# Reordering the expert-routing work on VectorE inside an attention loop

## Chip, cores and metric

One core of a Trainium2 chip runs the whole program in one launch. The metric is the device time of that launch in microseconds (us). Its engines are TensorE (PE), with its weight loads (PEld), VectorE (DVE), ScalarE (ACT), GpSimd (POOL) and SyncE (SP, which only issues transfers here). Each engine works through its own instructions in program order and meets the others at semaphores.

## What is computed

16 sequences of 256 tokens of width 128 go through one layer of a transformer in float32:

```
x = x + attention(layernorm(x))          # 16 heads of 64
x = x + experts(layernorm(x))
# experts: 160 experts of inner width 64, 8 of them for each token
probs = sigmoid(x @ router_w.T + expert_bias)
top_w, top_idx = top_k(probs, 8);  top_w = 2.5 * top_w / sum(top_w)
routed = sum over the 8 of  top_w * (silu(x @ w_gate[e].T) @ w_down[e].T)
shared = silu(x @ w_gate_shared.T) @ w_down_shared.T
```

## The kernel before

The program has two parts. The first goes over the sequences and does attention and routing. The second multiplies blocks of 64 rows by their expert's weights and adds up eight results for each token. The change lies in the first part alone.

The first part is one pipeline written as the same loop on each engine, `body(b)`, which `sequences` calls for b = 0 to 18: b = 0 to 3 written out, 4 to 15 as a hardware loop, 16 to 18 written out. A body has eight steps g = 0 to 7, one for each pair of heads; steps count on as 8b + g. The pipeline is skewed. In step g PE makes queries and keys of this step's heads (psY, L397), transposes the probabilities of three steps ago (psT, L431), multiplies the result of four steps ago by the output weights (psA, L443), then makes the scores of one step ago (psS, L406) and the probabilities times values of three steps ago (psO, L483). On even steps it also makes values (psVM, L397). In the middle of that order, before psS, stand the routing's own products: the counts over the tokens' masks at g = 0, the transposes of the second layer norm's output (psVM, L456) at g = 4, the router's logits and the next input's transposes at g = 6.

One step's chain through the other engines: DVE takes the negated row maxima of the scores (negmax, L1118); ACT takes four exponentials with them (p_sb, L675, with the row sums); DVE takes the reciprocal of the sums at the top of the next step (rinv, L1073) and scales a quarter of the probabilities (L1076), POOL two quarters (L789) and ACT one (L667). ACT's order in a step is: copy of psY (L651), the two copies of the transposed probabilities psT to pT_sb (L279, which psO waits for), the copy of the values on odd steps (L658), its quarter (L667), and then the four exponentials; at g = 5 also a copy to xn2T_res (L680). DVE's order in a step is: rinv, its quarter, a first group of other work, negmax, the copy of psO to oT_sb (L1124), and a second group of other work. PE takes psS only when the four exponentials of the step before are done, because they read the same bank.

The other work on DVE is the layer norms and the routing. With b the loop's number, the second layer norm of sequence b - 1 has its statistics at g = 3 (after the residual add into x_res, L1095) and is applied at g = 4 (xn, L894); between them POOL takes the inverse deviation (ve L760, rs L762). The routing of sequence b - 2 (`seq(b, 2)`) is spread out thus: `distances` and `new_blocks` at g = 0, `slot_numbers` at g = 1 before negmax, `best_slots` at g = 1 after it, `new_state` and `chosen` at g = 2 before negmax, `best_places` at g = 2 after it, `blocks` at g = 4 after it, `weights` at g = 5 before it. `best_slots` finds for each token its eight row numbers (slot_u, L992); from g = 1 on POOL scatters the tokens' rows there with 16 indirect transfers a sequence (`scatter`, L829), in order: 1, 2, 1, 2, 2, 3, 3 at g = 1 to 7, and 2 at the next body's g = 0. Before writing slot_u, DVE waits until all scatters of the sequence before have landed (semaphore scat); POOL waits for the same before it copies the next rows to xn2_src (L795). `new_state` carries the block state forward, `chosen` and `best_places` find expert numbers with max_index, `weights` computes the eight normalised weights.

The functions touched by the diff:

Of the kernel before, what the change touches and what calls it, by code (L numbers as in the profile page):

```python
# [66 lines left out]
def build(nc, x, wq, wk, wv, wo, bo, rwT, ebias, wgd, wgsT, wdsT, out):  # L67
# [4 lines left out]
    with ExitStack() as ctx:  # L72
# [6 lines left out]
        def wait(eng, s, value):  # L79

            if not isinstance(value, int) or value > 0:
                eng.wait_ge(s, value)
# [3 lines left out]
        def wait_apart(eng, s, value):  # L86


            if isinstance(value, int):
                wait(eng, s, value)  # L90
            else:
                eng.reg_mov(held[eng], value)
                eng.wait_ge(consts, 5)
                eng.wait_ge(s, held[eng])
# [151 lines left out]
        def live(b, g, lag, last=NSTEP):  # L246


            return not isinstance(b, int) or 0 <= G * b + g - lag < last

        def seq(b, lag):
            return not isinstance(b, int) or 0 <= b - lag < B

        def is_last(b, lag):


            return isinstance(b, int) and b - lag == B - 1
# [618 lines left out]
        def _(dve):  # L876
# [13 lines left out]
            def ln_apply(b, which, dst, mv, rs):  # L890
                wait(dve, s[which + "_rs"], b + 1)
                for i in range(TB):
                    src = x_res[:, bass.ds(b * TB + i, 1), :].rearrange("p o d -> p (o d)")
                    dve.tensor_scalar(dst[:, i, :], src, mv[:, i, 0:1], rs[:, i:i + 1], ALU.subtract,  # L894
                                      ALU.mult).then_inc(s[which + "_xn"], 1)

            def input_split(b):

                wait(dve, s["xt_ps"], b + 1)
                wait(dve, s["v_ps"], G // 2 * b)  # L900
                wait(dve, s["yq_ps"], G * b)
                dve.tensor_copy(xnT_hi[:], psO[:, 0, SEQ:2 * SEQ]).then_inc(s["xt_hi"], 1)
                wait(dve, s["xt_hi"], b + 1)
                dve.tensor_tensor(xnT_lo[:], psO[:, 0, SEQ:2 * SEQ], xnT_hi[:].bitcast(F32), ALU.subtract).then_inc(s["xt_lo"], 1)
# [66 lines left out]
            def slot_numbers(b):  # L971
# [7 lines left out]
                wait(dve, s["mv_ok"], n)  # L979
                wait(dve, s["dq_ok"], n)  # L980
                dve.tensor_tensor(placed[:], placed[:], moved[:], ALU.add).then_inc(s["pl_ok"], 1)

            def best_slots(b):
                n = b - 1
                wait_apart(dve, s["pl_ok"], n)
                for i in range(TB):
                    m = dve.max(slot8[:, i, :], placed[:, i, :])
                m.then_inc(s["s8_ok"], 1)
                wait(dve, s["s8_ok"], n)
                if not is_last(b, 2):  # L990
                    wait(dve, s["scat"], 16 * TB * TOPK * (b - 2))
                dve.tensor_scalar(slot_u[:, int(is_last(b, 2))], slot8[:], -(MARK / HB + HALF_UP), float(HB), ALU.add, ALU.mult).then_inc(s["su_ok"], 1)  # L992

            def new_state(b):
                n = b - 1
                dve.scalar_tensor_tensor(out=newest[:], in0=nb_new[:], scalar=0.5, in1=taken[:], op0=ALU.is_gt,
                                         op1=ALU.mult).then_inc(s["nw_ok"], 1)
                wait(dve, s["nw_ok"], n)
                dve.tensor_tensor(last_blk[:], last_blk[:], newest[:], ALU.max).then_inc(s["st_ok"], 1)
                dve.tensor_copy(n_taken[:], taken[:, E - 1:E]).then_inc(s["st_ok"], 1)  # L1000

            def chosen(b):
# [3 lines left out]
                m.then_inc(s["eo_ok"], 1)  # L1006
                wait(dve, s["su_ok"], n)
                dve.tensor_copy(pos_u[:, bass.ds((b - 2) * TB, TB), :], slot_u[:, int(is_last(b, 2))]).then_inc(s["pu_ok"], 1)

            def best_places(b):  # L1010
                for i in range(TB):
                    m = dve.max_index(top_i[:, i, :], top_s[:, i, :], score[:, i, :])
                m.then_inc(s["ti_ok"], 1)
# [47 lines left out]
            def body(b):  # L1061
                for g in range(G):
                    step = G * b + g
                    if g == 4 and seq(b, 1):
                        wait(dve, s["x2t_ps"], b - 1)
                        wait(dve, s["xs_ok"], b - 1)
                        ln_apply(b - 1, "ln2", xn2, mv2, rs2)
                    if live(b, g, 2):
                        u = step - 2
                        wait(dve, s["p_ok"], 4 * u + 4)  # L1070
                        wait(dve, s["pn_ok"], 2 * u - 2)
                        wait(dve, s["pna_ok"], u - 1)
                        dve.reciprocal(rinv[:, (g - 2) % 2], rowsum[:, (g - 2) % 2]).then_inc(s["ri_ok"], 1)  # L1073
                        wait(dve, s["ri_ok"], u + 1)
                        pq = p_sb[:, (g - 2) % 2, 0, 0, :]
                        dve.tensor_scalar(pq, pq, rinv[:, (g - 2) % 2, 0, 0:1], None, ALU.mult).then_inc(s["pnd_ok"], 1)  # L1076
                    if g == 7 and live(b, g, 0):
                        input_split(b + 1)

                    if seq(b, 2):  # L1080
                        if g == 0:
                            distances(b)
                        if g == 1:
                            slot_numbers(b)
                        if g == 2:
                            new_state(b)
                            chosen(b)
                        if g == 5:
                            weights(b)
                    if seq(b, 1):  # L1090
                        if g == 3:
                            wait(dve, s["ao_ps"], G * b)
                            wait(dve, s["xb_ok"], b)
                            xr = x_res[:, bass.ds((b - 1) * TB, TB), :]
                            dve.tensor_tensor(xr, psA[:, 0, 0:SEQ].rearrange("p (i d) -> p i d", i=TB), xr, ALU.add).then_inc(s["x1_ok"], 1)  # L1095
                            ln_stats(b - 1, "ln2", st2, mv2)
                        if g == 6:
                            if isinstance(b, int) and b == 1:
                                dve.wait_ge(s["c_in"], 16 * (4 + 2 * TB))
                            wait(dve, s["lg_ps"], b)  # L1100
                            wait(dve, s["ez_ok"], b - 1)
                            dve.tensor_tensor(z_sb[:], psVM[:, 0, 0:TB * E].rearrange("p (i e) -> p i e", i=TB), eb_sb[:], ALU.add).then_inc(s["z_ok"], 1)
                        if g == 7:
                            best(b)
                    if g == 4 and live(b, g, 0):
                        if isinstance(b, int) and b == 0:
                            dve.wait_ge(s["x_in"], 16)
                        ln_stats(b + 1, "ln1", st1, mv1)
                    if g == 5 and live(b, g, 0):
                        wait(dve, s["xt_ps"], b + 1)  # L1110
                        ln_apply(b + 1, "ln1", xn1, mv1, rs1)

                    if live(b, g, 1):
                        u = step - 1
                        wait(dve, s["p_ok"], 4 * u - 4)
                        for h in range(2):
                            wait(dve, s["s_ps"], 2 * u + h + 1)
                            dve.tensor_reduce(negmax[:, (g - 1) % 2, h, :], psS[:, h, :].rearrange("p (i k) -> p i k", i=TB),  # L1118
                                              AX.X, ALU.max, negate=True).then_inc(s["nm_ok"], 1)
                    if live(b, g, 3):  # L1120
                        u = step - 3
                        wait(dve, s["o_ps"], u + 1)
                        wait(dve, s["ao_ps"], u - 1)
                        dve.tensor_copy(oT_sb[:, (g - 3) % 2, :], psO[:, 0, 0:SEQ]).then_inc(s["ot_ok"], 1)  # L1124

                    if seq(b, 2):
                        if g == 0:
                            new_blocks(b)
                        if g == 1:
                            best_slots(b)  # L1130
                        if g == 2:
                            best_places(b)
                        if g == 4:
                            blocks(b)
                    if g == 7 and seq(b, 1):
                        choose(b)

            sequences(dve, body)


# [112 lines left out]
```

## Time and profile before

| | |
|---|---|
| median of 3 runs | 1104.22 us (1103.38 to 1104.33) |
| the profiled execution, its own time | 1104.33 us |
| its span in the trace | 1102.4 us |
| PE busy | 831.2 us, 75% |
| DVE busy | 758.8 us, 69% |
| POOL busy | 704.4 us, 64% |
| ACT busy | 673.1 us, 61% |

The span is the time from the first to the last record; 1.9 us of the execution's time lie around it. Busy shares are averages over both parts of the program. The attention part covers the first 650 us or so, the experts the rest.

### The profile page before, as it was taken

The page shows a single profiled execution, that of the slowest core. Times are in us where ns is not written, and L with a number is a line of the kernel's source. Part 1 is how long each engine was busy: PE and PEld are TensorE (multiplying, and loading weights), DVE is VectorE, ACT ScalarE, POOL GpSimd, SP SyncE. Part 2 cuts the span into 40 slices and gives each one's busy share as a digit, 9 for nine tenths or more (in the row PEclk, how much of TensorE's full clock was granted, in tenths as well). Part 3 has the DMA queues.
Part 4 walks back from the last instruction along what each step waited for, and adds up shares of the span by engine and source line. Part 5 has one row for each costly group of instructions (what it writes and reads, how often), then busy time and mean ns, then how long its engine had stood idle before and what let it go on. Part 6 is the DMA issues. An engine that isn't in the chain of part 4 may idle for free.

```text
span 1102.4 us, 28627 instructions
## 1 busy us (share of the span) xinstructions
PE 831.2 (75%) x8062; PEld 640.1 (58%) x8062; DVE 758.8 (69%) x2574; ACT 673.1 (61%) x1997; POOL 704.4 (64%) x892
## 2 busy tenths in 40 slices
PE   4999999999999999999999968899776770000000
PEld 4777777777777777777777744677565560000000
DVE  4568878778887887887877875577887884223223
ACT  5888888888888888888888851377664550000000
POOL 2235677676776667767667667103777777777775
PEclk9999999999999999999999995699998885555555
DMA  8814422323333311221212123388887762112111
GB/s 261 328 40 157 154 106 100 144 109 133 143 143 120 118 64 62 75 84 65 93 64 68 55 110 151 129 268 278 284 254 228 227 223 76 57 57 57 57 57 50
DMA packets 62457, 144.61 MB, mean 131 GB/s; under 512 B 12496, under 2 KB 18576, under 8 KB 62416
## 3 DMA queue, kind: packets, MB, share of 16 engines
q1 hardware_dynamic: 46032, 110.56, 28.5%
q0 software_dynamic: 16384, 33.59, 10.0%
q8 instruction: 16, 0.26, 0.1%
q14 instruction: 25, 0.20, 0.1%
HBM read 59.16 MB, written 84.93 MB: 131 GB/s over the span
## 4 chain that ended last, share of the span: by engine, by line
PE 57%; POOL 17%; issue 11%; DMA 6%; DVE 6%; ACT 2%; DVEq 1%; SPq 0%; POOLq 0%; ACTq 0%
POOL yg L852 14%; PE psS L406 11%; PE psO L483 10%; PE psT L431 8%; PE psY L397 8%; PE psVM L397 5%; PE psA L443 4%; DMA block_y<-y_b 4%; PE psS L604 2%; POOL slot_x L829 2%; PE psT L553 1%; PE psT L594 1%; DMA xb<-slot_x 1%; DVE w_b L1183 1%; ACT y_b L724 1%
## 5 line engine op out<-in xcount | busy, mean ns | idle before, releaser
L852 POOL DMA_INDIRECT yg<-block_y,tok_idx x256 | 252.1, 985 | 137.6 <-issue 79.0
L829 POOL DMA_INDIRECT slot_x<-xn_src,slot_u x240 | 244.0, 1017 | 99.2 <-issue 52.7
L675 ACT ACTIVATE p_sb<-psS,negmax 128x256 f32<-128x256 f32 x512 | 236.0, 473 | 95.8 <-DVE negmax L1118 93.8
L789 POOL TENSOR_SCALAR p_sb<-p_sb,rinv 128x256 f32<-128x256 f32 x256 | 138.9, 550 | 128.4 <-DVE rinv L1073 125.9
L1118 DVE TENSOR_REDUCE negmax<-psS 128x2 f32<-128x512 f32 x256 | 164.2, 682 | 37.5 <-PE psS L406 37.3
L1183 DVE COPY w_b<-w_all 128x192 f32 x672 | 135.1, 272 | 34.7 <-issue 30.5
L406 PE MATMUL psS<-qk_sb 64*128 64x256 f32 x1024 | 145.2, 402 | 2.6 <-ACT p_sb L675 2.6
L483 PE MATMUL psO<-pT_sb,v_sb 128*64 128x256 f32 x1024 | 138.8, 391 | 7.5 <-issue 5.5
L279 ACT COPY pT_sb<-psT 128x512 f32<-128x512 f32 x256 | 140.5, 615 | 1.4 <-PE psT L431 1.4
L431 PE MATMUL psT<-ident,p_sb 128*128 128x128 f32 x1024 | 132.7, 272 | 0.0
L1190 DVE TENSOR_TENSOR yg<-yg,wE_res 128x1024 f32<-128x1024 f32 x32 | 39.1, 1222 | 126.5 <-DMA yg<-block_y,tok_idx 126.0
L431 PEld LDWEIGHTS psT<-ident,p_sb 128*128 128x128 f32 x1024 | 114.8, 140 | 1.2 <-issue 0.8
L483 PEld LDWEIGHTS psO<-pT_sb,v_sb 128*64 128x64 f32 x1024 | 65.1, 136 | 67.0 <-issue 36.8
L675 ACT ACTIVATION_READ_ACCUMULATOR p_sb<-psS,negmax 128x1 f32 x512 | 104.0, 203 | 0.0
L406 PEld LDWEIGHTS psS<-qk_sb 64*128 64x128 f32 x1024 | 88.5, 186 | 25.3 <-issue 7.8
L604 PE MATMUL psS<-xbT,w_b 128*64 128x64 f32 x1344 | 62.8, 241 | 34.1 <-issue 25.6
L651 ACT COPY qk_sb<-psY 128x512 f32<-128x512 f32 x128 | 76.1, 595 | 7.3 <-PE psY L397 4.9
L604 PEld LDWEIGHTS psS<-xbT,w_b 128*64 128x64 f32 x1344 | 51.2, 149 | 50.6 <-issue 44.5
L443 PE MATMUL psA<-wo_sb,oT_sb 128*128 128x128 f32 x512 | 79.5, 278 | 0.5 <-DVE oT_sb L1124 0.5
L667 ACT ACTIVATE p_sb<-p_sb,rinv 128x256 f32<-128x256 f32 x128 | 71.0, 555 | 0.0
L443 PEld LDWEIGHTS psA<-wo_sb,oT_sb 128*128 128x128 f32 x512 | 67.2, 191 | 2.0 <-DVE oT_sb L1124 1.0
L1073 DVE RECIPROCAL rinv<-rowsum 128x4 f32<-128x4 f32 x128 | 22.7, 177 | 66.3 <-ACT p_sb L675 62.8
(159 smaller groups left out, 1720.3 us busy)
## 6 DMA issues: line engine op xcount, KB each, us to landing
block_y<-zero SPq DMA_DIRECT2D x21, 1024.0 KB, 4.0
xb<-slot_x SPq DMA_DIRECT2D x84, 256.0 KB
block_y<-y_b SPq DMA_DIRECT2D x84, 256.0 KB
w_all<-in_wgd_dram SPq DMA_DIRECT2D x16, 960.0 KB
slot_x<-zero SPq DMA_DIRECT2D x1, 11264.0 KB, 40.9
slot_x<-zero SPq DMA_DIRECT2D x10, 1024.0 KB
yg<-block_y,tok_idx POOLq DMA_INDIRECT x256
slot_x<-xn_src,slot_u POOLq DMA_INDIRECT x240
```

What stands on the lines that cost most here:

```text
L279: copy(pT_sb[:, (g - 3) % 2, h].rearrange("p a t -> p (a t)"), psT[:, h, :]).then_inc(s[f"pt{h}_ok"], 1)
L397: m = pe.matmul(dst, wsl[a], xsl[c], start=(n == 0), stop=(n == 2))
L406: m = pe.matmul(psS[:, h, qt * SEQ:(qt + 1) * SEQ], qk_sb[r, par, 0, qt * P:(qt + 1) * P], qk_sb[r, par, 1, :], start=True, stop=True)
L431: m = pe.transpose(psT[:, h, kt * SEQ + qt * P:kt * SEQ + (qt + 1) * P], p_sb[:, (g - 3) % 2, h, qt, kt * P:(kt + 1) * P], ident[:])
L443: m = pe.matmul(psA[:, 0, i * P:(i + 1) * P], oT_sb[:, (g - 4) % 2, i * P:(i + 1) * P], wo_sb[:, gp, :], start=(gp == 0 and i == 0), stop= ...
L483: m = pe.matmul(psO[h * DH:(h + 1) * DH, 0, 0:SEQ], v_sb[:, (g - 3) // 2 % 2, kt, (g - 3) % 2, h * DH:(h + 1) * DH], pT_sb[:, (g - 3) % 2, ...
L675: act.activation(p_sb[:, (g - 1) % 2, h, qt, :], psS[:, h, qt * SEQ:(qt + 1) * SEQ], ACT.Exp, bias=negmax[:, (g - 1) % 2, h, qt:qt + 1], s ...
L789: pool.tensor_scalar(pq, pq, rinv[:, (g - 2) % 2, k // 2, k % 2:k % 2 + 1], 1.0, ALU.mult, ALU.mult).then_inc(s["pn_ok"], 1)
L829: pool.indirect_dma_start(slot_x, bass.IndirectOffsetOnAxis(ap=slot_u[:, int(last), i, j:j + 1], axis=0), (xn2 if last else xn2_src)[:, i, ...
L852: pool.indirect_dma_start(yg[:, r, k, :], None, block_y, bass.IndirectOffsetOnAxis(ap=tok_idx[:, par, r, k:k + 1], axis=0)).then_inc(gat[r ...
L1118: dve.tensor_reduce(negmax[:, (g - 1) % 2, h, :], psS[:, h, :].rearrange("p (i k) -> p i k", i=TB), AX.X, ALU.max, negate=True).then_inc(s ...
L1183: m = dve.tensor_copy(w_b[:, r, i, :], w_all[:, bass.ds(e, 1), :].rearrange("p o i -> p (o i)"))
```

## The change

The text of `best_slots` becomes the end of `slot_numbers`, so that it runs at g = 1 ahead of negmax. `new_state` moves from g = 2 ahead of negmax to g = 1 behind negmax and the oT copy. The text of `best_places` becomes the end of `chosen`, at g = 2 ahead of negmax. `weights` moves from g = 5 to g = 3, where it stands ahead of the residual add and the statistics. No instruction is added or removed. The order of the other engines' programs is the same.

```diff
@@ -979,9 +979,6 @@
                 wait(dve, s["mv_ok"], n)
                 wait(dve, s["dq_ok"], n)
                 dve.tensor_tensor(placed[:], placed[:], moved[:], ALU.add).then_inc(s["pl_ok"], 1)
-
-            def best_slots(b):
-                n = b - 1
                 wait_apart(dve, s["pl_ok"], n)
                 for i in range(TB):
                     m = dve.max(slot8[:, i, :], placed[:, i, :])
@@ -1006,8 +1003,6 @@
                 m.then_inc(s["eo_ok"], 1)
                 wait(dve, s["su_ok"], n)
                 dve.tensor_copy(pos_u[:, bass.ds((b - 2) * TB, TB), :], slot_u[:, int(is_last(b, 2))]).then_inc(s["pu_ok"], 1)
-
-            def best_places(b):
                 for i in range(TB):
                     m = dve.max_index(top_i[:, i, :], top_s[:, i, :], score[:, i, :])
                 m.then_inc(s["ti_ok"], 1)
@@ -1083,9 +1078,8 @@
                         if g == 1:
                             slot_numbers(b)
                         if g == 2:
-                            new_state(b)
                             chosen(b)
-                        if g == 5:
+                        if g == 3:
                             weights(b)
                     if seq(b, 1):
                         if g == 3:
@@ -1127,9 +1121,7 @@
                         if g == 0:
                             new_blocks(b)
                         if g == 1:
-                            best_slots(b)
-                        if g == 2:
-                            best_places(b)
+                            new_state(b)
                         if g == 4:
                             blocks(b)
                     if g == 7 and seq(b, 1):
```

## Rows read from the trace of the kernel before

**Rows 1.** Busy time (and instructions) of PE, PEld, DVE, ACT, POOL; granted clock; DMA by stretch.

```profile
core 0: us, PE busy (x) PEld busy (x) DVE busy (x) ACT busy (x) POOL busy (x), PEclk, DMA share, GB/s
300.00:340.00 40.00, 39.42 (x317) 30.80 (x313) 32.36 (x109) 33.91 (x105) 28.16 (x40) 1.00 0.35 131
...
640.00:650.00 10.00, 8.16 (x69) 5.87 (x66) 9.19 (x27) 6.78 (x23) 7.46 (x10) 1.00 0.10 33
...
660.00:665.00 5.00, 1.53 (x5) 1.04 (x4) 4.26 (x24) 1.25 (x3) 3.84 (x4) 0.50 1.02 409
```

**Rows 2.** Waits on PE and PEld, 62 to 619 us: total, times, longest.

```profile
PE psO L483 <- issue: 4.9, 16, 0.4
...
PEld psO L483 <- ACT pT_sb L279: 10.8, 16, 0.8
```

**Rows 3.** PE in time order: start, duration, instruction, [idle before <- releaser].

```profile
335.24 1.08 PE L483 MATMUL psO<-pT_sb,v_sb 128*64 128x256 f32 x8
...
345.28 1.08 PE L483 MATMUL psO<-pT_sb,v_sb 128*64 128x256 f32 x8
...
355.84 1.08 PE L483 MATMUL psO<-pT_sb,v_sb 128*64 128x256 f32 x8 [0.30 <-issue]
```

**Rows 4.** ACT in time order, at g = 2 of one body and g = 5 of another.

```profile
334.03 1.11 ACT L279 COPY pT_sb<-psT 128x512 f32<-128x512 f32 x2
...
632.67 0.41 ACT L680 COPY xn2T_res<-xn2T 128x256 f32 x1
```

**Rows 5.** DVE in time order, g = 1 to g = 3 of one body.

```profile
330.44 0.68 DVE L981 TENSOR_TENSOR placed<-placed,moved 128x320 f32<-128x320 f32 x1
331.04 1.27 DVE L1118 TENSOR_REDUCE negmax<-psS 128x2 f32<-128x512 f32 x2
...
332.57 0.54 DVE L987 MAX8 slot<-placed 128x8 f32<-128x160 f32 x2
333.24 0.17 DVE L992 TENSOR_SCALAR slot_u<-slot 128x16 uint32<-128x16 f32 x1
333.87 0.18 DVE L1073 RECIPROCAL rinv<-rowsum 128x4 f32<-128x4 f32 x1 [0.46 <-ACT p_sb L675]
...
334.36 0.32 DVE L996 SCALAR_TENSOR_TENSOR newest<-nb_new,taken 128x160 f32<-128x160 f32 x1
...
335.01 0.08 DVE L1005 MATCH_VALUE_LOAD e_of<-slot,placed 128x8 f32 x1
...
335.79 1.27 DVE L1118 TENSOR_REDUCE negmax<-psS 128x2 f32<-128x512 f32 x2
...
338.62 0.18 DVE L1073 RECIPROCAL rinv<-rowsum 128x4 f32<-128x4 f32 x1 [0.64 <-ACT p_sb L675]
...
339.43 0.42 DVE L1095 TENSOR_TENSOR x_res<-psA,x_res 128x256 f32 x1 [0.23 <-PE psA L443]
...
340.80 1.29 DVE L1118 TENSOR_REDUCE negmax<-psS 128x2 f32<-128x512 f32 x2
```

**Rows 6.** DVE in time order, g = 3 and g = 5 of the body before.

```profile
299.78 0.42 DVE L1095 TENSOR_TENSOR x_res<-psA,x_res 128x256 f32 x1 [0.24 <-PE psA L443]
...
309.50 0.24 DVE L1040 RECIPROCAL top_w<-top_s 128x16 f32<-128x16 f32 x1
...
311.17 0.61 DVE L894 TENSOR_SCALAR xn<-x_res,mv,rs 128x128 f32 x2
311.70 1.27 DVE L1118 TENSOR_REDUCE negmax<-psS 128x2 f32<-128x512 f32 x2
```

**Rows 7.** POOL in time order, two bodies: inverse deviation at g = 3, rows' copy at g = 1.

```profile
342.07 0.18 POOL L760 TENSOR_SCALAR ve<-mv 128x2 f32<-128x2 f32 x1
...
412.14 0.41 POOL L795 TENSOR_SCALAR xn_src<-xn 128x256 f32<-128x256 f32 x1 [0.81 <-DMA slot_x<-xn_src,slot_u]
```

**Rows 8.** DVE in time order, g = 1 of the body of the second row of Rows 7.

```profile
410.99 0.68 DVE L981 TENSOR_TENSOR placed<-placed,moved 128x320 f32<-128x320 f32 x1
```

**Rows 9.** DVE, then POOL, in time order at g = 3 of b = 16.

```profile
654.34 0.25 DVE L887 BATCH_NORM_AGGREGATE mv<-st 128x2 f32<-128x6 f32 x2
...
657.59 0.19 POOL L760 TENSOR_SCALAR ve<-mv 128x2 f32<-128x2 f32 x1
```

## Prediction

> **What bounds the kernel now.** The change touches only DVE's order in the attention part, so I read that part first by stretches of one sequence. In 40 us PE is busy 39.42 us at a granted clock of 1.00 (full speed, 2.4 GHz), DVE 32.36 and ACT 33.91 [rows 1]. PE is the bound, and DVE has about 7 us of idle time a sequence. From one residual add to the next, 299.78 to 339.43, a sequence takes 39.65 us [rows 5, 6]; a stall of PE adds to that, anything else is free.
>
> Then the waits of PE, to see what already stalls it. psO waits about 0.3 us 16 times, and its weight load waits for the pT_sb copies of ACT 16 times [rows 2]. So the place at which DVE and ACT touch PE is psO: it cannot start before ACT has copied the transposed probabilities, and ACT does those copies only after the four exponentials of the step before, which wait for negmax. Last the order in time, to measure how close each step runs. At g = 2 the pT_sb copies end at 334.03 + 1.11 = 335.14, and psO starts at 335.24 [rows 3, 4]: nothing is to spare there. From negmax of g = 1 (331.04) to that psO are 4.20 us. I use this as the rule of the sum: **psO of a step cannot start sooner than 4.20 us after negmax of the step before.** It gives 335.79 + 4.20 = 339.99 for g = 3 and 340.80 + 4.20 = 345.00 for g = 4, where psO started at 345.28 [rows 3, 5]; g = 4 has 0.28 us to spare. For g = 6, 311.70 + 39.65 = 351.35 is negmax of g = 5 in the later body; with 4.20 and some 0.3 us for the copy L680, which ACT does only there, it gives 355.85, and the row has 355.84 with a stall of 0.30 us [rows 3, 4, 6]. The rule fits both places where PE is held.
>
> A second rule closes the loop: rinv of a step starts 2.83 us after negmax of the step before, when ACT is waited for (331.04 to 333.87, 335.79 to 338.62) [rows 5].
>
> **The change, part by part.** No work is added, so every term is a delay or an advance of a negmax.
>
> *g = 1, best slots ahead of negmax.* Today two MAX8 and slot_u follow behind the oT copy, 332.57 to 333.24 + 0.17. In the new order the MAX8 can start only when the add into placed is done (330.44 + 0.68 = 331.12), slot_u 0.67 later (as 332.57 to 333.24), and negmax some 0.15 us after that: about 331.95 in place of 331.04 [rows 5]. That is 0.91 us later. Behind negmax new_state takes the place of best_slots; it needs 334.36 to 335.01, 0.65 us, where best_slots took 0.84, and DVE idled 0.46 us after that until ACT let it take rinv. ACT's exponentials hide it, so it costs nothing; without them it would cost its 0.65 us. psO of g = 2 comes at 331.95 + 4.20 = 336.15, which is **0.91 us of PE stall** where 0 stood.
>
> *g = 2.* Here negmax loses new_state ahead of it (0.65 us) and gains the max_index pairs of best_places. The same four instructions in chosen, with the small copy of pos_u, take 335.01 to 335.79, 0.78 us in all; I take 0.67 for the four alone. So rinv is at 331.95 + 2.83 = 334.78 and negmax at 334.78 + (335.79 - 333.87) - 0.65 + 0.67 = 336.72, late by 0.93. psO of g = 3 is bound for 340.92, and PE, 0.91 late, is not held again. Nothing more is lost or won.
>
> *g = 3, weights.* The eight small instructions of weights took 309.50 to 311.17, 1.67 us [rows 6]. They go in front of the residual add. rinv is at 336.72 + 2.83 = 339.55. From rinv to negmax are now 340.80 - 338.62 = 2.18 us, of which 0.23 is a wait for psA [rows 5] that weights would cover. negmax: 339.55 + 1.95 + 1.67 = 343.17, late by 2.37. psO of g = 4: 343.17 + 4.20 = 347.37 in place of 345.28, late by 2.09, so **1.18 us more**. The second layer norm is also late: its statistics are ready about 2.4 us later, and POOL, which took them up at 342.07 [rows 7] after a scatter although they were ready at 340.80, now waits for DVE. Its result is then back before DVE has finished negmax and the oT copy of g = 3, so the apply (L894) and PE's transposes of it come some 1.6 us late, still inside the 2.09 of psO. They run beside the other delay and add nothing.
>
> *g = 4 and 5.* Negmax of g = 4 carries at most the 2.37 us. At g = 5 it had been held by weights; without their 1.67 us it is ready as soon as PE's scores are. So the stall of 0.30 us at g = 6 goes [rows 3]: **0.30 us back**. From g = 6 on DVE again waits for PE, and nothing of the lateness is carried into the next sequence.
>
> *The scatters.* DVE now waits for the last sequence's scatters before negmax, so a late landing would hold negmax. In six sequences POOL waited for that landing, longest until 412.14 [rows 7]. There the add started at 410.99 [rows 8], and by the interval of rows 5 (330.44 to about 331.82) slot_u would be due at 412.37. The landing is 0.23 us earlier: cost 0, but 1 for 1 from there. slot_u comes about 1.4 us sooner for POOL's first scatter. POOL is on no path of PE at that step, so I give that nothing.
>
> *The end of the part.* At b = 16 there is no negmax. The weights' 1.67 and the 0.91 us delay statistics that were done at 654.34 + 0.25 and taken up by POOL only at 657.59 [rows 9]: 3.0 us of cover for 2.6. Cost 0.
>
> **Sum.** 0.91 + 1.18 - 0.30 = 1.79 us a sequence. Routing runs together with full attention for b = 2 to 15, 14 sequences: 25.1 us. The profiled execution took 1104.33 us, 0.11 above the median: 1104.33 + 25.1 = **1129.4 us**.
>
> **Rivals.**
>
> *A, the insertions are partly hidden.* Either of the two costs might be smaller than the rule says, if what is late at ACT is caught up. With only g = 1 paying, 0.91 - 0.30 = 0.61 us, 8.5 us in all: 1112.9. With only g = 3, 0.88 us, 12.3 in all: 1116.7. For it speaks the idle time of ACT and DVE, some 6 and 7 us a sequence; against it, that ACT's copies end 0.10 us before psO.
>
> *B, both are paid in full and nothing comes back.* 0.91 + 1.67 = 2.58 us, 36.1 in all: 1140.4. It needs the stall at g = 6 to stay, and the 0.28 us to spare at g = 4 and the 0.23 us wait for psA to be of no use, as they would be if scatters landing later held slot_u.
>
> *C, faster.* One mechanism: weights gone from g = 5 ends the 0.30 us stall, and both insertions are hidden. 14 x 0.30 = 4.2 us less: 1100.1. It decides at psO of g = 2: the copies would have to end 0.9 us before it, and they end 0.10 us before it [rows 3, 4].
>
> *D, PE's clock.* The new stalls, 0.9 and 1.2 us, might make the chip grant the low clock. The trace is against it: 640 to 650 us has PE busy 8.16 of 10 us and the clock is 1.00; it is 0.50 (1.2 GHz) only at 660 to 665, where PE is busy 1.53 of 5 us [rows 1]. Were one step of a sequence, 39.65 / 8 = 4.96 us, run at half the clock, that would be 14 x 4.96 = 69 us more: about 1199. The Trainium skill (TensorE: Matmul & The Clock Gate, What's actually happening) says that the engine's clock is halved after it has been idle and restored by activity; by that rule this rival would need much longer idle stretches than these, and the trace agrees as far as it goes.
>
> *E, no change.* A loss of just the stall's size. Only an accident of A would give it: 1104.
>
> **How the numbers follow.** Sum as worked out 0.68, its own range 1124 to 1135 (1.4 to 2.2 us a sequence); A 0.13; B 0.10; C 0.05; D 0.02; E 0.02. The range takes in A and B: 1112 to 1141. About 0.2%, 2.2 us, is what a measurement of this kernel can tell from no change. Faster has C, 0.05; same has E, 0.02; slower has the rest, 0.93.
>
> **What would show it.** In the trace after, a sequence should take about 41.4 us from residual add to residual add. The psO waits of PE should sit at g = 2 (about 0.9 us) and at g = 4 (about 1.2, perhaps shared with a wait of psS for the exponentials), and be gone at g = 6. Negmax of g = 3 should start about 3.6 us after rinv, against 2.18. A psO still back to back at g = 2 would prove A; a wait of slot_u for scatters, or a stall left at g = 6, B. The forecast is wrong if the 4.20 us from negmax to psO shrink when ACT runs late, since ACT has idle time in it that I take as fixed.

## The result, and the profile after

The changed kernel takes 1123.02 us (median of 4 runs, 1120.68 to 1125.95) beside 1104.28 us for the kernel before: a ratio of 1.0171, 95% interval 1.0141 to 1.0201. It is slower by about 19 us. The forecast was slower, 1129.4 us in a range of 1112 to 1141: direction right, size a third too large (25.1 us forecast, 18.7 measured). A second comparison gave 1123.16 beside 1103.62, a ratio of 1.0177 (1.0154 to 1.0199).

First the stretch of a sequence. In 41 us PE is now busy 39.02 us, at the same granted clock of 1.00; before, it was 39.42 of 40 [rows 1].

```profile
core 0: us, PE busy (x) PEld busy (x) DVE busy (x) ACT busy (x) POOL busy (x), PEclk, DMA share, GB/s
300.00:341.00 41.00, 39.02 (x309) 30.34 (x307) 32.30 (x106) 33.44 (x103) 27.66 (x38) 1.00 0.34 128
```

Two residual adds of the kernel after, one body apart (L1095 before is L1089 here), stand 41.47 us apart; before it was 39.65 [rows 5, 6].

```profile
310.30 0.42 DVE L1089 TENSOR_TENSOR x_res<-psA,x_res 128x256 f32 x1
...
351.77 0.42 DVE L1089 TENSOR_TENSOR x_res<-psA,x_res 128x256 f32 x1
```

The growth is 1.82 us a sequence, where the sum of the prediction had 1.79. The waits of PE from 62 to 640 us (total, times, longest) show what took the time: psO's own wait has grown from 4.9 to 9.4 us [rows 2]; psA now waits for DVE's copy to oT_sb, which it did not before; and psS waits for ACT's exponentials 16 times, where it did once before, for 0.2 us.

```profile
PE psO L483 <- issue: 9.4, 27, 0.4
PE psA L443 <- DVE oT_sb L1118: 9.1, 12, 0.8
PE psS L406 <- ACT p_sb L675: 5.3, 16, 0.5
```

A third wait is gone. The kernel before held PE also at g = 4, ahead of the transposes of the second layer norm's output (62 to 619 us, then one case of it in time order):

```profile
PE psVM L456 <- DVE xn L894: 4.3, 11, 1.5
...
343.85 0.44 PE L456 MATMUL psVM<-ident,xn 128*128 128x128 f32 x2 [0.28 <-DVE xn L894]
```

PE in time order, kernel after: g = 2 (first four rows), g = 4 (next five) and g = 6 (last two).

```profile
301.05 1.04 PE L431 MATMUL psT<-ident,p_sb 128*128 128x128 f32 x8
302.11 0.71 PE L443 MATMUL psA<-wo_sb,oT_sb 128*128 128x128 f32 x4
303.15 1.14 PE L406 MATMUL psS<-qk_sb 64*128 64x256 f32 x8 [0.33 <-ACT p_sb L675]
304.65 1.08 PE L483 MATMUL psO<-pT_sb,v_sb 128*64 128x256 f32 x8 [0.36 <-issue]
...
311.50 1.03 PE L431 MATMUL psT<-ident,p_sb 128*128 128x128 f32 x8
313.35 0.71 PE L443 MATMUL psA<-wo_sb,oT_sb 128*128 128x128 f32 x4 [0.81 <-DVE oT_sb L1118]
313.89 0.41 PE L456 MATMUL psVM<-ident,xn 128*128 128x128 f32 x2
314.39 1.13 PE L406 MATMUL psS<-qk_sb 64*128 64x256 f32 x8
315.88 1.08 PE L483 MATMUL psO<-pT_sb,v_sb 128*64 128x256 f32 x8 [0.36 <-issue]
...
324.91 1.14 PE L406 MATMUL psS<-qk_sb 64*128 64x256 f32 x8
325.98 1.08 PE L483 MATMUL psO<-pT_sb,v_sb 128*64 128x256 f32 x8
```

The reader should see a stall at g = 2, a stall at g = 4 in several pieces, and none at g = 6, where psO follows psS by 1.07 us without idle time; before, 0.30 us of idle stood there [rows 3]. To measure each by the same yardstick I take the time from the start of the transposes (psT) to the start of psO. At g = 2 it went from 2.53 us (332.71 to 335.24 in the trace of before) to 3.60, at g = 4 from 3.20 (342.08 to 345.28) to 4.38, at g = 6 from 3.72 (352.12 to 355.84) to 3.24 (322.74 to 325.98). That is 1.07 + 1.18 - 0.48 = 1.77 of the 1.82 us.

DVE in time order, kernel after, g = 1 to g = 3, and negmax of g = 5.

```profile
298.76 0.68 DVE L981 TENSOR_TENSOR placed<-placed,moved 128x320 f32<-128x320 f32 x1
299.54 0.55 DVE L984 MAX8 slot<-placed 128x8 f32<-128x160 f32 x2
300.23 0.17 DVE L989 TENSOR_SCALAR slot_u<-slot 128x16 uint32<-128x16 f32 x1
300.44 1.29 DVE L1112 TENSOR_REDUCE negmax<-psS 128x2 f32<-128x512 f32 x2
...
303.29 0.18 DVE L1068 RECIPROCAL rinv<-rowsum 128x4 f32<-128x4 f32 x1 [0.58 <-ACT p_sb L675]
...
305.20 1.26 DVE L1112 TENSOR_REDUCE negmax<-psS 128x2 f32<-128x512 f32 x2
...
308.02 0.18 DVE L1068 RECIPROCAL rinv<-rowsum 128x4 f32<-128x4 f32 x1 [1.23 <-ACT p_sb L675]
...
308.50 0.25 DVE L1035 RECIPROCAL top_w<-top_s 128x16 f32<-128x16 f32 x1
...
311.67 1.29 DVE L1112 TENSOR_REDUCE negmax<-psS 128x2 f32<-128x512 f32 x2
...
321.01 1.29 DVE L1112 TENSOR_REDUCE negmax<-psS 128x2 f32<-128x512 f32 x2 [0.39 <-PE psS L406]
```

The rule of the prediction can be checked against the PE rows: negmax of g = 1 at 300.44, psO of g = 2 at 304.65, 4.21 us; negmax of g = 3 at 311.67, psO of g = 4 at 315.88, 4.21 us. The rule holds elsewhere too: between 180 and 600 us the traces of all fourteen runs have 80 to 84 steps each, and in none of them did a psO start less than 4.18 us after the negmax of the step before. And rinv comes 2.85 and 2.82 us after negmax, where 2.83 was said. From rinv to negmax at g = 3 are 3.65 us, against 2.18 [rows 5] and the 3.6 forecast. Negmax of g = 5 now waits for PE.

**Where the rest of the 25 us is.** 14 intervals between residual adds grew. Twelve of them grew by 1.6 to 1.9 us. Two grew only by 0.76 and 0.73: those from b = 2 to 3 and from b = 9 to 10, which took 40.14 and 40.92 us already before. In the first PE was already held twice at g = 2 before the change (0.24 us at psS, 0.27 at psO). In the second the wait for the layer norm's output was 1.52 us long, and the later psO of the changed kernel hides it:

```profile
384.74 0.44 PE L456 MATMUL psVM<-ident,xn 128*128 128x128 f32 x2 [1.52 <-DVE xn L894]
```

Together the intervals up to the last residual add (62.18 to 653.36 before, 62.98 to 677.23 after) grew by 23.1 us. The first add is 0.8 us later, before any moved work has run, and the rest of the execution, from the last add to the end, took 449.0 us before (1102.4 - 653.36) and 446.8 after (1124.0 - 677.23). 23.1 + 0.8 - 2.2 = 21.7 us, the difference of the two spans (1124.0 - 1102.4 = 21.6) but for rounding; the profiled execution after was a long one, 1125.83 us. The second pair of traces, runs e5 and e6 below, has the same pattern: 22.6 us more up to the last add (654.79, then 677.42), and 448.9 against 445.6 us behind it. The medians differ by 18.7 and 19.5 us; if the first part took the same time in the executions without a trace, 3 to 5 us came back behind it.

So in the traces 2.2 and 3.3 us came back in the second part, whose code is the same. In the first pair the shared expert's matmuls ran at different clocks. The kernel before, then after:

```profile
665.00:689.00 24.00, 23.24 (x59) 11.61 (x59) 12.71 (x49) 4.72 (x7) 18.21 (x19) 0.50 0.30 112
```

```profile
689.00:713.00 24.00, 19.92 (x97) 11.48 (x97) 15.35 (x53) 5.90 (x9) 18.21 (x20) 0.93 0.28 107
```

In the kernel before PE was granted half its clock (1.2 GHz) throughout, while busy 23.24 of 24 us; in the kernel after the clock was 1.00 (2.4 GHz) from 695 to 715 us. That did not decide the time, though. In e6, the changed kernel again, the clock was 0.50 from 700 to 725 us, and the first transposes of the second part's blocks (psT, L594) still started 46.1 us after the last residual add, against 45.9 in the first trace of the changed kernel, where PE sat idle for 10.98 us just before them and waited for a transfer. In the two traces of the kernel before these transposes started 47.8 and 46.2 us after the last residual add. So 1.9 us of the first pair and 0.1 us of the second came back ahead of them. What shortened the second part stays open.

### The profile page after: what moved, and what is told of

It is laid out like the page before. It is cut to its first block, busy times and chain, and to the rows that moved or that the text cites. A ratio compares the mean times of both kernels' runs of the same rounds, so it can differ in the third digit from the quotient of the medians.

```text
span 1124.0 us, 28627 instructions
## 1 busy us (share of the span) xinstructions
PE 826.6 (74%) x8062; PEld 634.5 (56%) x8062; DVE 765.3 (68%) x2574; ACT 671.9 (60%) x1997; POOL 705.8 (63%) x892
## 4 chain that ended last, share of the span: by engine, by line
PE 38%; POOL 16%; issue 15%; DVE 15%; DMA 7%; ACT 7%; DVEq 1%; ACTq 0%; POOLq 0%; SPq 0%
POOL yg L852 13%; PE psS L406 8%; PE psO L483 6%; ACT p_sb L675 6%; DMA block_y<-y_b 5%; PE psT L431 5%; PE psY L397 5%; DVE negmax L1112 3%; PE psVM L397 3%; POOL slot_x L829 3%; PE psA L443 3%; PE psS L604 2%; PE psT L594 2%; ACT y_b L724 1%; PE psO L615 1%
## 5 line engine op out<-in xcount | busy, mean ns | idle before, releaser
L594 PE MATMUL psT<-ident,xb 128*128 128x128 f32 x336 | 60.4, 307 | 18.0 <-DMA xb<-slot_x 17.6
```

## The experiments

Five other orders were run, four of them two or three times, because the chip turned out to matter: the kernel before took 1103.62 us on one chip, and 1257.5, 1248.9 and 1257.4 us on three others (called the slower chips below). All five orders ran on the slower chips alone. Each run was compared with the kernel before on its own chip. The kernel before was not traced on a slower chip. Theory T is the prediction's rule, that psO starts no sooner than 4.20 us after the negmax before it and that a late negmax is paid in full.

**The kernels themselves again (e5, e6).** No edit.

> The kernel before, unchanged, on the chip of this call, for its trace. If PE sets the pace here as in the trace of before, 39.65 us a sequence and about 1104. If this chip has stalls of its own in PE's program, as the four runs before this one suggest (their kernel before took 1257.5), the psO stall at g = 6 is covered by other gaps, a sequence takes more than 40.5 us, and DVE's order matters less.

> The changed kernel, unchanged, on the chip of this call. Theory T, where PE sets the pace: 41.46 us a sequence and a ratio of 1.017 again. Rival A, where PE is held by something else: the sum of what the two parts cost alone on such a chip (0.0013 and 0.0082), a ratio of about 1.009.

Measured: e5 one execution, 1105.57 us, a sequence 39.67 us; e6 1123.16 us, ratio 1.0177 (1.0154 to 1.0199), a sequence 41.46 us. Theory T's number on a chip where PE sets the pace. In the steady sequences the step lengths of e5 and e6 agree with those of the first two traces within 0.04 us.

**best_slots alone (e1, e7, e11).**

```diff
                         if g == 1:
                             slot_numbers(b)
+                            best_slots(b)
...
-                        if g == 1:
-                            best_slots(b)
                         if g == 2:
                             best_places(b)
```

> The kernel before with one part of the change: best_slots at g = 1 ahead of negmax; new_state, best_places and weights stay where they were. Theory T (psO starts no sooner than 4.20 us after the negmax before it, and a late negmax is paid in full beyond what is to spare): psO at g = 2 stalls 0.91 us, the 0.30 us stall at g = 6 stays; 39.65 + 0.91 = 40.56 us a sequence, 12.7 us in all, about 1117. Rival A (partly hidden): the psO at g = 2 is held by less than half of it, under 40.1 us a sequence, under 1111.

> The same kernel as e1 (best_slots ahead of negmax at g = 1, nothing else), now wanted beside a kernel before of about 1104. Theory T: psO at g = 2 stalls 0.91 us, the 0.30 us stall at g = 6 stays: 40.56 us a sequence, 12.7 us in all, a ratio of 1.0115. Rival A: under 40.1 us a sequence, a ratio under 1.006.

> The same kernel as e1 and e7 (best_slots ahead of negmax at g = 1, nothing else), for a chip on which the kernel before takes about 1104; on the two chips of 1249 and 1257 it cost nothing that could be told. In the trace of the changed kernel the stretch from PE's transposes to psO at g = 2 grew by 1.07 us. Theory T: the same here, with the stall at g = 6 kept: 40.7 us a sequence, 13 to 14 less what sequences with holds of their own hide: a ratio of 1.011 to 1.013. Rival A: a ratio under 1.006.

Measured: ratios 1.0013 (0.9997 to 1.003), 1.0007 (0.9989 to 1.0026) and 1.0004 (0.9981 to 1.0026). By the total, rival A's number three times. But the trace shows the stall that T wants. e11, PE in time order at g = 2 and g = 3:

```profile
469.71 1.13 PE L406 MATMUL psS<-qk_sb 64*128 64x256 f32 x8 [0.32 <-ACT p_sb L675]
471.20 1.08 PE L483 MATMUL psO<-pT_sb,v_sb 128*64 128x256 f32 x8 [0.36 <-issue]
...
474.63 0.61 PE L443 MATMUL psA<-wo_sb,oT_sb 128*128 128x128 f32 x4
```

e11, DVE in time order: the negmax of g = 1 before it, and the residual add behind psA.

```profile
467.00 1.29 DVE L1119 TENSOR_REDUCE negmax<-psS 128x2 f32<-128x512 f32 x2
...
475.40 0.42 DVE L1096 TENSOR_TENSOR x_res<-psA,x_res 128x256 f32 x1
```

471.20 - 467.00 = 4.20 us, the rule to the hundredth, and nearly the same two idle times (0.32 and 0.36 us) as in the changed kernel. The stall is in the trace, and the total does not show it. From the third on, the sequences took 41.0 to 42.5 us in the three runs, against T's 40.56 and 40.7, which were worked out from the faster chip.

**weights alone (e2, e8).**

```diff
-                        if g == 5:
+                        if g == 3:
                             weights(b)
```

> The kernel before with the other part alone: weights at g = 3 ahead of the residual add. Theory T: negmax of g = 3 is late by 1.67 - 0.23 = 1.44 us, 0.28 of it to spare, so 1.16 us at g = 4, and 0.30 us come back at g = 6; 40.51 us a sequence, 12.0 us in all, about 1116. If the order of the two parts matters (that weights cost only because g = 1 is late as well), under 40.1 us a sequence, under 1111. Where PE is held at g = 4: by psO waiting for ACT if T's path is the one; by psA waiting for the oT_sb copy if that comes first.

> The same kernel as e2 (weights at g = 3 ahead of the residual add, nothing else), beside a kernel before of about 1104. Theory T: 1.16 us more at g = 4, 0.30 us back at g = 6: 40.51 us a sequence, 12.0 us in all, a ratio of 1.0109. Rival A: under 40.1 us a sequence, a ratio under 1.006. If psA waiting for the oT_sb copy is only the first place at which the same lateness is seen, psA and psO at g = 4 together are held 1.2 us.

Measured: 1.0082 (1.0059 to 1.0106) and 1.0019 (1.0001 to 1.0036). The first is 9.5 us, four fifths of T's 12 us, the second 1.6 us. It is the same order on two slower chips: in e2 four early sequences took 42.9 to 43.0 us, in e8 the same four took 41.5 to 42.2. What makes the difference was not found. e2, DVE in time order at g = 3:

```profile
313.67 0.55 DVE L1044 TENSOR_TENSOR eq<-e_of,top_i 128x128 f32<-128x128 uint32 x1
...
314.25 0.61 DVE L1049 TENSOR_TENSOR eqw<-eq,top_w 128x128 f32<-128x128 f32 x1
...
316.99 0.69 DVE L1118 TENSOR_REDUCE negmax<-psS 128x2 f32<-128x512 f32 x1
```

e2, PE in time order at g = 4:

```profile
318.66 0.71 PE L443 MATMUL psA<-wo_sb,oT_sb 128*128 128x128 f32 x4 [1.15 <-DVE oT_sb L1124]
...
321.20 1.08 PE L483 MATMUL psO<-pT_sb,v_sb 128*64 128x256 f32 x8 [0.36 <-issue]
```

321.20 - 316.99 = 4.21 us again. Most of the lateness is seen first at psA (1.15 us): PE's product with the output weights needs the oT_sb copy, which DVE makes right behind negmax. It is the same lateness, not a second one, since psO still starts where negmax puts it.

**The changed kernel with weights back (e3).**

```diff
-                        if g == 3:
+                        if g == 5:
                             weights(b)
```

> The changed kernel with weights put back at g = 5. Theory T: what is left is the 0.91 us of g = 1, and the 0.30 us stall at g = 6 is back; 40.56 us a sequence as in the run with the slots alone, about 1117; the exchange of new_state and best_places costs nothing, so the two runs differ by less than 0.1 us a sequence. Rival B (something else of the new order costs as well): more than 40.7 us a sequence.

Measured: 1.0016 (0.9995 to 1.0036), beside 1.0013 for e1 on the same chip. Between the two, no difference that can be told, as T had it: exchanging new_state and best_places costs nothing that this chip shows. But the 12.7 us that T gave to each of the two runs are not there on this chip.

**Taking PE's stalls away (e4, e9: weights behind negmax; e10, e12: also the scatter of g = 3 behind the inverse deviation).**

```diff
-                        if g == 5:
-                            weights(b)
...
                         if g == 4:
                             blocks(b)
+                        if g == 5:
+                            weights(b)
```

and on GpSimd, for e10 and e12 alone,

```diff
-                    if not is_last(b, 1) or g != 3:
+                    if g != 3:
                         scatter(b, g)
                     if g == 3 and seq(b, 1):
                         inverse_deviation(b - 1, "ln2", mv2, ve2, rs2)
-                    if is_last(b, 1) and g == 3:
+                    if g == 3:
                         scatter(b, g)
```

> The kernel before with weights at g = 5 behind negmax and the oT_sb copy, in DVE's idle time. Theory T: negmax of g = 5 waits for PE alone, the 0.30 us stall of psO at g = 6 goes and nothing is paid for it: 39.35 us a sequence, 4.2 us less in all, about 1100. If the stall at g = 6 is not of DVE's making (of ACT's copy to xn2T_res alone): 39.65 us, 1104.

> The same kernel as e4 (weights at g = 5 behind negmax and the oT_sb copy), beside a kernel before of about 1104. Theory T, and the mechanism of rival C by itself: the 0.30 us stall of psO at g = 6 goes at no price, 39.35 us a sequence, 4.2 us less in all, a ratio of 0.996. If the stall at g = 6 is ACT's own, 39.65 us and 1.000.

> The kernel before with weights at g = 5 behind negmax, and on GpSimd at g = 3 the inverse deviation ahead of the scatter instead of behind it. The second takes aim at PE's other stall, 0.28 us before the transposes of xn at g = 4. Theory T: both go, 39.65 - 0.30 - 0.28 = 39.07 us a sequence, 8.1 us less in all, about 1096. If psO at g = 4 then waits for ACT (negmax of g = 3 + 4.20 us = 345.00 against 345.28), the second gives the 0.28 us just so; if the scatter's lateness comes back in GpSimd's scaling at g = 4, only 4.2 us less or nothing.

> The same kernel as e10 (weights at g = 5 behind negmax; inverse deviation ahead of the scatter at g = 3), for such a chip. Theory T: 39.65 less 0.30 to 0.48 at g = 6 and less 0.28 at g = 4: 38.9 to 39.1 us a sequence, 8 to 10 us less in all, a ratio of 0.991 to 0.993. If only the stall at g = 6 can go (psO at g = 4 bound by ACT): 0.995 or 0.996.

Measured: e4 1.0003 (0.9987 to 1.0019), e9 0.9999 (0.9983 to 1.0015), e10 0.9991 (0.9975 to 1.0007), e12 0.9999 (0.9977 to 1.0021). In all four traces psO at g = 6 follows psS by 1.06 or 1.07 us in every sequence with routing, without the 0.30 us stall. The right comparison is with e1, e7, e11 and e3, which ran on the same chips and have weights ahead of negmax at g = 5. There most sequences have 1.13 to 1.16 us, with PE late already from g = 2 on, but the first two with routing have 1.50 to 1.52 and one in the middle 1.43 or 1.44, with the stall in place. PE in time order at g = 6 of that one, e11 and then e12, both on the same chip:

```profile
408.99 1.08 PE L483 MATMUL psO<-pT_sb,v_sb 128*64 128x256 f32 x8 [0.29 <-issue]
```

```profile
401.83 1.08 PE L483 MATMUL psO<-pT_sb,v_sb 128*64 128x256 f32 x8
```

So the stall was of DVE's making. What GpSimd's edit did shows at the long hold between b = 9 and 10: the step from g = 3 to g = 4 took 6.3 us in e4 and e9, and 5.1 in e10 and e12, because PE's wait for xn there, 1.56 and 1.55 us in e4 and e9, is 0.35 us in e10 and nothing in e12. But nothing came of either in the total: T's ratios of 0.996 and of 0.991 to 0.993 were missed. Whether these two orders are faster on a chip of 1104 us could not be tried; T's estimate of 1096 to 1100 stands untested.

**What the slower chips do.** e12, all engines in time order, around the residual add of g = 3:

```profile
467.17 0.61 PE L443 MATMUL psA<-wo_sb,oT_sb 128*128 128x128 f32 x4
...
468.95 0.42 DVE L1093 TENSOR_TENSOR x_res<-psA,x_res 128x256 f32 x1 [1.25 <-PE psA L443]
```

DVE waited 1.25 us for a product that by PE's record began at 467.17 and lasted 0.61 us: 1.78 us from its start to the add. In the trace of before the same two starts are 0.78 us apart (338.65 and 339.43, [rows 5]), with DVE waiting for the product there too. In e11, on e12's own chip but behind a stall of PE, they are 0.77 us apart (474.63 to 475.40 above), and DVE did not wait. In e4, e9, e10 and e12 this distance is 1.66 to 1.81 us in every steady sequence but one, and 0.77 in that one, which comes behind the long hold between b = 9 and 10. The same is seen at g = 7. e12, all engines in time order:

```profile
487.07 0.28 PE L397 MATMUL psY<-xnT_hi,wk_lo 128*128 128x256 f32 x1
...
488.67 0.59 ACT L651 COPY qk_sb<-psY 128x512 f32<-128x512 f32 x1 [0.91 <-PE psY L397]
...
490.33 1.08 PE L483 MATMUL psO<-pT_sb,v_sb 128*64 128x256 f32 x8 [0.59 <-ACT pT_sb L279]
```

There ACT waited 0.91 us for keys whose last product began 1.60 us earlier. On all three slower chips step 7, from its psS to the next one, takes 4.9 to 7.0 us in nearly every steady sequence, where it took 4.65 in the kernels before and after, and the median sequence of e4, e9, e10 and e12 is 41.0 to 41.4 us long, on the scale of the slowed kernel after. In these traces PE's results reach the others up to 1 us late once PE has gone some steps without a stall, and on time behind one. That is as if PE's true pace were behind its recorded starts there, with a stall eating a backlog instead of time. It would explain why 1.07 us of recorded stall at g = 2 cost nothing. It is argued, not shown: the profile records where matmuls start and models their ends, and the granted clock is 1.00 on both kinds of chip. Nor do the runs tell a slow chip from a slow moment, as none of these chips was seen both slow and fast.

## Why the prediction was right, point by point

*PE bounds the part, and DVE touches it through negmax.* The way is shown by the traces: the 4.20 us from negmax to the next psO held in the kernel after (4.21, 4.21), in e11 (4.20) and in e2 (4.21). The price of each part is shown only by the step lengths of the changed kernel; the runs with one part alone fell on the slower chips, where even the stalls that are in the trace were not paid in full in the total. The fear named last in the prediction, that this time shrinks when ACT runs late, was unfounded: behind negmax ACT has exponentials and copies without a gap.

*g = 1: 0.91 forecast, 1.07 measured.* MAX8 started 0.10 us after the end of the add, where the prediction had it start at once, slot_u 0.69 behind it in place of 0.67, and negmax 0.21 behind slot_u's start in place of 0.15. Negmax came 2.29 us after psS against 1.21: 1.08 later. A term mis-sized by 0.16.

*g = 2: nothing.* Right: psO of g = 3 followed psS by 1.06 us. That new_state and best_places cost nothing is shown by e3 beside e1 only on a chip that hides much.

*g = 3: 1.18 forecast, 1.18 measured* from transposes to psO. What the prediction did not name is where the lateness shows first: 0.81 us of it at psA, waiting for the oT_sb copy, before psO. It does not add, because psO is later still. The prediction also counted two places where PE was held and missed a third, the 0.28 us ahead of the transposes at g = 4. It took these 0.28 us as time to spare for psO, which was right in the sum: the wait is gone in the kernel after, because xn is ready before PE gets there. DVE's copy behind negmax is a second way from negmax to PE that was there to be seen in the code. Weights itself took 1.80 us (308.50 to 310.30) up to the start of the residual add, 0.13 more than the 1.67 of the prediction, but 0.33 us of it went into the gap ahead of that add, where 0.23 was counted; the work in front of negmax grew by 1.47, with 1.44 forecast. In e2 the same instructions took 2.12 us (313.50 to 315.62). The product of two SBUF tensors eqw takes 0.29 us while GpSimd runs no such arithmetic (661.23 in the trace of before), 0.45 in the kernel after, where the last part of GpSimd's scaling (308.37 to 309.42) runs beside it, and 0.61 in e2, where it lies wholly beside the scaling (314.24 to 315.21). The comparison eq is longer in e2, too, 0.55 against 0.41, and its record ends before the scaling starts; that part is not explained. The Trainium skill (GPSIMD Engine Reference, 1. Specifications) says that GpSimd and VectorE share their SBUF interfaces and contend when a VectorE instruction has two SBUF inputs; the three times of eqw agree.

*g = 6: 0.30 back forecast, 0.48 measured.* 0.37 of it between psS and psO, 0.11 ahead of psS. Mis-sized by 0.18, and it offsets the error at g = 1, so that the sum of a sequence, 1.79, was met at 1.82 partly by luck.

*14 sequences at 25.1 us in all: 23.1 measured.* This is 2.0 us of the miss of 6.4 us. The steady sequence was multiplied by 14 although two of the intervals, at 40.14 and 40.92 us, had holds of their own and grew by less than half. They could have been found before by listing all intervals and not one.

*The scatters, cost 0.* Once they did cost something. In the interval from b = 9 to 10 slot_u waited for the last scatters to land, and the step there took 5.18 us in place of 5.00; the trace of e6 has no such wait. DVE in time order, kernel after:

```profile
424.78 0.18 DVE L989 TENSOR_SCALAR slot_u<-slot 128x16 uint32<-128x16 f32 x1 [0.32 <-DMA slot_x<-xn_src,slot_u]
```

*Nothing in the rest.* Here is the larger part of the miss: 2.2 and 3.3 us came back behind the last residual add in the two pairs of traces, and 3 to 5 us by the medians. The prediction had 0 there. Its cover of 3.0 us at b = 16 held: the interval up to the last residual add took 35.12 us before and 35.08 after, and PE's transposes of xn (L456) started 6.10 us behind that add before and 5.85 after. The executions of the kernel after spread over 5.3 us, those of before over 2.0, while the first parts of the two traces of the changed kernel agree within 0.2 us. Since what shortened the second part is open, so is how much of this miss is chance.

*The rivals.* A did not hold in the two comparisons near 1104 us; on the slower chips something like it did (1.0013, 1.0007 and 1.0004 for the first part alone). B is out: the stall at g = 6 went. C's mechanism was real, its 0.30 us stall went in e4 and e9 at no price, but both insertions were paid. D is out: the clock was 1.00 throughout the attention part (60 to 640 us).

## What to carry to other kernels

Where one engine is saturated, measure for each result that it waits for the fixed time from the instruction that another engine can be late with (here negmax) to the instruction that is held (here psO), and compare it with the present distance; here what was moved ahead of the first was paid one for one beyond the difference, and idle time of the other engines did not help. Multiply by the number of periods only after looking at every period. And an effect of one per cent has to be taken apart on the same kind of chip as the question: the order that cost 1.7% beside a kernel of 1104 us has a first part that cost nothing measurable on three slower chips.

## What the runs showed of the hardware that was not expected

The same kernel took 1104.28 and 1103.62 us in two comparisons, and 1249 to 1257 us on three other chips. No trace of the kernel before was taken on those; the orders that ran there had a granted clock of 1.00 through the attention part, as it had, yet a median sequence of 41.0 to 41.7 us in place of its 39.65. Behind the last residual add e12 took 579 us against 449, and there the clock was lower: 0.79 from 713 to 800 us and 0.68 from 800 to 900, against 0.98 and 0.86 in the kernel before. Within the kernel before PE was granted half its clock from 660 to 705 us, although it was busy all of the time from 675 to 700 us; the kernel after had full clock from 695 to 715 us, in the same matmuls.
